# A two-layer convolution and attention block on one core: a new table of steps, rounded scores, a select on GpSimd and an FFN begun by halves

## The reference

```python
x = x + conv_attention(group_norm(x, 32 groups))   # rms norm over channels, 4 heads of 32, softmax over all 256 tokens
t = to_tokens(x)                                   # [4, 256, 64]
t = t + attention(layer_norm(t))                   # 4 heads of 16, causal mask, biases
t = t + moe_ffn(layer_norm(t))                     # 8 experts, 64 -> 256 -> 64, exact gelu, gate takes the top 2
x = from_tokens(t)
```

## Time and profile before

| | |
|---|---|
| median of 3 runs | 114.58 us |
| profiled execution, its own time | 114.85 us |
| its span (first to last instruction) | 112.8 us |
| PE busy | 101.8 us (90%) |
| DVE busy | 75.4 us (67%) |
| ACT busy | 65.1 us (58%) |
| GpSimd busy | 15.8 us (14%) |
| chain that ended last | PE 68%, DVE 16%, ACT 10%, issue 3% |
| granted clock of TensorE, mean | 0.998 |

### The profile page before, as it was taken

One profiled execution on the slowest core, in us unless ns is written; L12 is line 12 of the kernel. 1 busy time (PEld: TensorE's weight loads), 2 busy tenths in 40 slices (PEclk: granted clock), 3 DMA queues, 4 the chain that ended last, 5 costly groups with the idle time before them and its releaser, 6 DMA issues.

```text
span 112.8 us, 2251 instructions
## 1 busy us (share of the span) xinstructions
PE 101.8 (90%) x831; PEld 52.8 (47%) x831; DVE 75.4 (67%) x210; ACT 65.1 (58%) x121; POOL 15.8 (14%) x28
## 2 busy tenths in 40 slices
PE   5989978889899999997899998999999999999920
PEld 2346456655555455566666654675342323232300
DVE  6965899979505469999966688998638453155250
ACT  4039973433888756564329958894937644764400
POOL 7900200000000000000000000000003941343140
PEclk9999999999999999999999999999999999999999
DMA  2940000199700000000000000000000000000003
GB/s 74 246 84 7 2 0 9 31 237 189 118 0 0 0 9 0 0 0 0 6 0 6 0 0 0 0 0 3 0 6 0 0 0 0 0 0 0 0 0 93
DMA packets 6633, 3.16 MB, mean 28 GB/s; under 512 B 4432, under 2 KB 6496, under 8 KB 6624
## 3 DMA queue, kind: packets, MB, share of 16 engines
q1 hardware_dynamic: 5936, 2.38, 11.5%
q10 hardware_dynamic: 688, 0.66, 2.3%
HBM read 2.77 MB, written 0.26 MB: 27 GB/s over the span
## 4 chain that ended last, share of the span: by engine, by line
PE 68%; DVE 16%; ACT 10%; issue 3%; DVEq 0%; ACTq 0%
PE bank L933 13%; PE bank L944 13%; PE bank L874 6%; PE bank L807 6%; PE bank L839 5%; PE bank L888 4%; PE bank L858 4%; PE bank L749 3%; PE bank L758 3%; PE bank L721 2%; DVE mx L590 2%; DVE mx L586 2%; ACT sq L399 2%; PE bank L845 1%; ACT sq L405 1%
## 5 line engine op out<-in xcount | busy, mean ns | idle before, releaser
L481 ACT ACTIVATE hid<-bank,b1c 128x1024 f32<-128x1024 f32 x16 | 16.9, 1112 | 11.8 <-PE bank L933 11.8
L437 ACT ACTIVATE pr<-bank 128x1024 f32<-128x1024 f32 (+1 forms) x16 | 14.0, 914 | 8.5 <-PE bank L845 5.1
L933 PE MATMUL bank<-xn,w_sb 64*128 64x512 f32 x64 | 15.6, 612 | 0.0
L944 PE MATMUL bank<-hid,w_sb 128*64 128x512 f32 x64 | 15.3, 603 | 0.0
L705 DVE SCALAR_TENSOR_TENSOR yw<-bank,b2c,wc 128x512 f32<-128x512 f32 x8 | 6.0, 748 | 12.6 <-PE bank L944 12.6
L721 PE MATMUL bank<-still 128*128 128x512 bf16 (+1 forms) x41 | 11.8, 437 | 1.2 <-DVE still L495 1.2
L359 POOL TENSOR_TENSOR acc<-yw,x 64x512 f32<-64x512 f32 x1 | 1.3, 1269 | 72.1 <-DVE yw L705 72.1
L586 DVE TENSOR_REDUCE mx<-bank 128x4 f32<-128x1024 f32 x8 | 9.3, 1218 | 0.9 <-PE bank L807 0.8
L807 PE MATMUL bank<-k,q 32*128 32x256 f32 (+1 forms) x128 | 8.3, 373 | 1.6 <-ACT q L425 0.6
L933 PEld LDWEIGHTS bank<-xn,w_sb 64*128 64x128 f32 x64 | 5.6, 186 | 8.5 <-ACT hid L481 4.4
L364 POOL TENSOR_TENSOR acc<-acc,yw 128x512 f32<-128x512 f32 x6 | 7.6, 1274 | 11.8 <-DVE yw L705 11.6
(11 more groups left out here) (148 smaller groups left out, 176.4 us busy)
## 6 DMA issues: line engine op xcount, KB each, us to landing
w_sb<-in_L_ffn_W_dram SPq DMA_DIRECT2D x3, 512.0 KB, 7.2
x<-in_x_dram ACTq DMA_DIRECT2D x2, 256.0 KB, 4.8
xg<-in_x_dram SPq DMA_DIRECT2D x1, 256.0 KB, 3.2
wg<-in_L_conv_w_qkv_dram SPq DMA_DIRECT2D x2, 96.0 KB, 4.8
bqkv<-in_L_attn_b_qkv_dram SPq DMA_DIRECT2D x12, 0.1 KB, 1.6
wo1t<-in_L_attn_W_out_dram SPq DMA_DIRECT2D x8, 4.0 KB, 1.8
out_dram<-acc SPq DMA_DIRECT2D x1, 128.0 KB, 2.5
out_dram<-acc ACTq DMA_DIRECT2D x1, 128.0 KB, 2.8
```

The costliest lines, as they stand in the source:

```text
L437: nc.scalar.activation(pr[:, b, 2 * p:2 * p + 2, 0:n], two(key, 0, n), ACT.Exp, scale=SCALE[l]).then_inc(free(key), 1)
L481: nc.scalar.activation(hid[:, k % 4, :, :], two(("h", 0, k)), ACT.Gelu, bias=b1c[:, k:k + 1]).then_inc(free(("h", 0, k)), 1)
L933: i = mm(ps(key, i=s), w1_sb[r, e, P * j:P * j + P], XN[r, 2 * s:2 * s + 2, :].rearrange("p b t -> p (b t)"), start=True, stop=True)
L944: i = mm(ps(key, p0=C * s, p1=C * s + C), w2_sb[:, k, :], hid[:, k % 4, s, :], start=(j == 0), stop=(j == FT - 1))
```

## The change

The table of steps is new in every place and bank, and has a further column with the number of zero matmuls ahead of a step. Beside that:

- Queries and keys are copied a second time, to a rounded 32-bit format (fp32r), by GpSimd (steps `qr`, `kr`, tiles Qr and Kr). `scores` uses these; `again` goes on with the float32 ones. So `scores` waits for `qr` and `kr`.
- `turn` becomes a matmul in fp32r with a rounded identity (a further cast on DVE in the set-up) in place of a float32 transpose.
- In layer 1 the mask matmuls of `again` (L845) are gone. After each exp, GpSimd sets the masked weights to zero by a select (steps `causal0`, `causal1`, 512 elements in each partition), and `num` waits for both. One of the two mask tables in the set-up is gone.
- In layer 0 the sums of rows have a bank of their own (`pd`), with a semaphore of its own, so `inv` can begin before `num` is done.
- The FFN works on the batches as 0, 2 (upper half) and 1, 3 (lower half). The first three `up` are cut into two halves of 256 columns. The first halves (`uphalf`) need batches 0 and 1 only and stand in the table, at 253, 260 and 263, ahead of the last gate at 264; the second halves follow after it.
- Zero matmuls: 13 at the start as before, then 26 in place of 28. 2 are ahead of the first `var`, 1 and 1 ahead of the first two `project`, 9 more in layer 0 (3 `scores`, 3 `turn`, 2 `again`, 1 `den`), 12 in layer 1 (7 `scores`, 1 `turn`, 4 `out`), and 1 ahead of a gate.
- `prep_rest` (PE) and the two ACT set-up copies are steps of the table now.

The diff, cut to its core:

```diff
 PLAN = (
...
-    ("xr", 0, (9, 14, 23, 31), ()),
-    ("xn", 0, (12, 18, 27, 39), ()),
-    ("project", 0, (16, 29, 35, 46), ((3, 4), (4, 3), (2, 0), (6, 7))),
-    ("q", 0, (21, 33, 37, 48), ()),
-    ("k", 0, (22, 36, 42, 49), ()),
-    ("scores", 0, (25, 40, 50, 53), ((0, 6), (6, 2), (4, 2), (6, 0))),
-    ("max0", 0, (32, 44, 52, 57), ()),
-    ("max1", 0, (34, 45, 54, 61), ()),
-    ("turn", 0, (38, 56, 60, 66), ((4,), (5,), (5,), (0,))),
+    ("xr", 0, (7, 21, 40, 44), (), ()),
+    ("xn", 0, (10, 24, 45, 46), (), ()),
+    ("project", 0, (12, 29, 47, 49), ((0, 4), (6, 7), (6, 7), (2, 3)), (1, 1, 0, 0)),
+    ("q", 0, (17, 32, 51, 58), (), ()),
+    ("k", 0, (16, 37, 50, 55), (), ()),
+    ("qr", 0, (19, 34, 53, 61), (), ()),
+    ("kr", 0, (22, 41, 56, 59), (), ()),
+    ("scores", 0, (25, 54, 67, 77), ((4, 0), (0, 6), (6, 4), (4, 0)), (3, 0, 0, 0)),
+    ("max0", 0, (28, 57, 69, 79), (), ()),
+    ("max1", 0, (33, 62, 71, 83), (), ()),
+    ("turn", 0, (38, 65, 75, 88), ((6,), (0,), (7,), (3,)), (2, 0, 1, 0)),
...
-    ("xn", 2, (212, 217, 226, 232), ()),
-    ("gate", 2, (218, 222, 230, 234), ((7,), (2,), (7,), (2,))),
-    ("logits", 2, (221, 231, 233, 235), ()),
+    ("xn", 2, (235, 246, 254, 259), (), ()),
+    ("gate", 2, (240, 251, 258, 264), ((0,), (0,), (5,), (5,)), (0, 0, 1, 0)),
+    ("logits", 2, (244, 261, 262, 265), (), ()),
+    ("uphalf", 2, (253, 260, 263), ((6,), (2,), (0,)), (0, 0, 0)),
 )
...
+            def causal(l, b, p):
+                emptied(pool, ("t", l, b, p))
+                diag = pr[:, b, 2 * p:2 * p + 2, :].rearrange("p h (n c) -> p h n c", c=P)[:, :, 0:3:2, :]
+                nc.gpsimd.affine_select(out=diag, in_=diag, compare_op=ALU.is_ge, fill=0.0, base=0,
+                                        pattern=[[0, 2], [0, 2], [1, P]], channel_multiplier=-1).then_inc(S["causal", p], 1)
+            def qr(l, b):
+                emptied(pool, ("yq", l, b))
+                nc.gpsimd.tensor_copy(Qr[:, b, :], Q[:, b, 0:T]).then_inc(S["qr", l], 1)
+            def kr(l, b):
+                emptied(pool, ("yk", l, b))
+                nc.gpsimd.tensor_copy(Kr[:, b, :], K[:, b, 0:T]).then_inc(S["kr", l], 1)
...
+            nc.vector.tensor_copy(identr[:, :], ident[:, :]).then_inc(cst, 1)
...
             def scores(l, b):
...
-                emptied(pe, ("yq", l, b))
-                emptied(pe, ("yk", l, b))
+                idle(("s", l, b, 0), ZEROS["scores", l][b])
+                pe.wait_ge(S["qr", l], b + 1)
+                pe.wait_ge(S["kr", l], b + 1)
...
-                        i = mm(bank_of("s", l, b, h)(c, c + n), Q[rows(h), b, P * q:P * q + P], K[rows(h), b, 0:n],
+                        i = mm(bank_of("s", l, b, h)(c, c + n), Qr[rows(h), b, P * q:P * q + P], Kr[rows(h), b, 0:n],
...
             def turn(l, b):
-                    i = nc.tensor.transpose(ps(key, P * q, P * q + P), mx[l][:, b, q, :, :].rearrange("p h c -> p (h c)"), ident[:, :])
+                    i = mm(ps(key, P * q, P * q + P), mx[l][:, b, q, :, :].rearrange("p h c -> p (h c)"), identr[:, :],
+                           start=True, stop=True)
...
             def again(l, b):
...
-                if l:
-                    for h in range(H):
-                        i = mm(blocks(bank_of("t", l, b, h)(0, L1)), identb[:, :], twice(cmask[:, 1, :]), start=False, stop=True,
-                               skip_group_check=True)
...
+            def up_part(k, n):
+                key = ("h", 0, k)
+                if n == 0:
+                    claim(pe, key)
+                    idle(key, ZEROS["uphalf", 2][k])
+                pe.wait_ge(ld["w1"], 32)
+                pe.wait_ge(S["xn", 2], 2 * n + 2)
+                e, j = divmod(k, FT)
+                for s in range(2):
+                    r = slice(C * s, C * s + C)
+                    i = mm(ps(key, T * n, T * n + T, i=s), w1_sb[r, e, P * j:P * j + P], XN[r, 2 * n + s, :],
+                           start=(n == 0), stop=True, skip_group_check=True)
+                if n:
+                    i.then_inc(full(key), 1)
...
-            up(0)
-            up(1)
+            for k in range(3):
+                up_part(k, 1)
             pe.wait_ge(ld["w2"], 16)
             for e in range(E):
-                if e + 1 < E:
+                if e == 0:
+                    up(3)
+                elif e + 1 < E:
```

More of the change, by code:

```diff
@@ L42 @@
[L42 to L52, removed]
@@ L63 @@
[L63 to L72, removed]
@@ new lines @@
+    ("inv", 0, (64, 85, 106, 122), (), ()),
+    ("weigh", 0, (66, 87, 110, 126), (), ()),
+    ("out", 0, (72, 90, 116, 129), ((6,), (2,), (0,), (7,)), (0, 0, 0, 0)),
+    ("resid", 0, (74, 92, 124, 132), (), ()),
+    ("center", 1, (78, 94, 127, 135), ((6,), (7,), (0,), (1,)), (0, 0, 0, 0)),
+    ("square", 1, (82, 97, 130, 141), (), ()),
+    ("var", 1, (91, 99, 131, 144), (), ()),
+    ("ln", 1, (98, 111, 133, 148), (), ()),
+    ("r", 1, (100, 113, 136, 150), (), ()),
+    ("r2", 1, (104, 115, 138, 155), (), ()),
@@ new lines @@
+    ("den", 1, (188, 199, 210, 223), (), ()),
+    ("inv", 1, (191, 203, 214, 227), (), ()),
+    ("weigh", 1, (193, 206, 219, 232), (), ()),
+    ("out", 1, (198, 211, 224, 236), ((4,), (5,), (6,), (6,)), (2, 0, 0, 2)),
+    ("resid", 1, (202, 216, 229, 239), (), ()),
+    ("center", 2, (207, 221, 230, 243), ((4,), (5,), (1,), (4,)), (0, 0, 0, 0)),
+    ("square", 2, (212, 225, 237, 245), (), ()),
+    ("var", 2, (215, 228, 238, 248), (), ()),
+    ("ln", 2, (218, 231, 241, 252), (), ()),
+    ("r", 2, (220, 233, 247, 255), (), ()),
@@ L102, in hybrid_block @@
     ORDER = [(step, l, b, banks[b] if banks else ()) for _, step, l, b, banks in
-             sorted((place[b], step, l, b, banks) for step, l, place, banks in PLAN for b in range(B))]
+             sorted((at, step, l, b, banks) for step, l, place, banks, _ in PLAN for b, at in enumerate(place))]
+    ZEROS = {(step, l): zeros for step, l, _, _, zeros in PLAN}
     seat, nth, follows = {}, {}, {}
@@ L124, in hybrid_block @@
             take(("norm", l, b), banks[0])
+        elif step == "prept":
+            take(("prep_t", 0), banks[0])
         elif step == "project":
@@ L133, in hybrid_block @@
         elif step in ("den", "num") and banks:
-            take(("pv", l, b), banks[0])
+            take(("pd" if step == "den" else "pv", l, b), banks[0])
         elif step == "out":
@@ L138, in hybrid_block @@
             take(("logits", l, b), banks[0])
-    for k in range(NK):
-        take(("h", 0, k), 2 * (k % 3), 2)
-    take(("gate_t", 0), 7)
+        elif step == "uphalf":
+            take(("h", 0, b), banks[0], 2)
+    for k in range(3, NK):
+        take(("h", 0, k), seat["h", 0, k % 3], 2)
+    last_pair = 12 - sum(seat["h", 0, k] for k in range(3))
+    take(("gate_t", 0), last_pair + 1)
     for e in range(E):
-        take(("y", 0, e), 6 + e % 2)
+        take(("y", 0, e), last_pair + e % 2)
     with ExitStack() as ctx:
@@ L635, in logits @@
                 emptied(dve, key)
-                for t in range(KT * b, KT * b + KT):
+                for t in range(first, first + KT):
                     i = nc.vector.max(m8[:, t, :], lg[:, t, :])
@@ L830, in again @@
                     claim(pe, ("t", l, b, p))
+                idle(("t", l, b, 0), ZEROS["again", l][b])
                 emptied(pe, ("turn", l, b))
+                emptied(pe, ("yq", l, b))
+                emptied(pe, ("yk", l, b))
                 if l == 0:
@@ L880, in out_ @@
                 claim(pe, key)
+                idle(key, ZEROS["out", l][b])
                 w = wo0t[:, :] if l == 0 else wo1t[:, :, :].rearrange("p r c -> p (r c)")
@@ L892, in gate @@
                 claim(pe, key)
-                idle(key, (2, 2, 4, 4)[b])
+                idle(key, ZEROS["gate", l][b])
                 pe.wait_ge(S["xn", l], b + 1)
```

180 lines of the change are left out of this document (104 added, 76 removed).

## The result

The changed kernel takes 115.38 us (median of 5, 115.26 to 115.60) against 114.65 for the kernel before: the ratio is 1.0058, 95% interval 1.004 to 1.0076. It is slower, by 0.7 us or 0.6%, small but clear of the interval, where I forecast 4.0 us faster. (Ratios here leave out executions that were more than 1.5% above the fastest of their kernel; where that hides something, single times are given.)

What follows compares the result with a forecast made beforehand. PE was taken to bound the kernel, with DVE level in two stretches. Terms -4.3 + 1.3 + 0.6 + 0.5 - 0.9 - 1.2 = -4.0 took 114.85 to 110.85, less 0.27: 110.6 us; range 106.8 to 114.2.

Steps and rivals of the forecast that it cites:

- What of this lands: PE's work to the end of layer 1: 6.2 us leave PE, of which 4.3 were counted as gained.
- its hops: GpSimd's new copies and selects between steps, and what GpSimd holds up on DVE: 0.6 us cost, bounds 0 and 4.
- the masks' 2.2 us: Mask of `again` in layer 1: 0.54 us four times off PE, three of four where PE sets the pace.
- Scores: fp32r scores steps: 0.55 us in layer 0, 0.45 in layer 1; 2.4 and 1.6 us saved on PE.
- Turn: Transposes as fp32r matmuls, eight steps: no change taken, bounds -2.1 to +3.0 us.
- Prologue: Start of batch 0: scores at 15.2 us in place of 14.36, first maxima about 0.2 later; +0.5 in the sum.
- Zero matmuls: 22 come in from the second `project` to the end of layer 1: 1.3 us cost, from 0 to 4.8.
- Rival D: Clock falls in the prologue, PE at half speed from 12 to 20 us: 115.6 us, chance 0.07.
- Halves: Three halves of `up` moved ahead of the last gate, free in place of zero matmuls: 1.2 us gained.
- the rest of the last stretch: From `out` of batch 3 to the first `up`, 6.97 us: 0.9 us gained, bounds 0 and 1.2.
- Rival C: GpSimd's copies and selects hold up two-input DVE instructions; at 10 us of delay 116.6 us, chance 0.07.

Runs made afterwards that it cites:

- z_all: Kernel before, old order, with all edits but the own bank for the sums, and 14 zero matmuls more: 114.58 us, ratio 0.9984.
- b_select: Kernel before with one edit: GpSimd's select in place of the mask matmuls of the second scores; 114.55 us, ratio 0.9985.
- n_f32: Changed kernel with its first scores back in float32, without the 16 GpSimd copies: 118.64 us, ratio 1.0366 to the kernel before.
- n_mask: Changed kernel with the second mask on PE again and no select: 116.53 us, ratio 1.0182 to the kernel before.
- n_zerohalves: Changed kernel with two zero matmuls in place of each first half, first three up matmuls whole behind the last gate: 115.73 us.
- n_kr: Changed kernel with kr of batch 0 ahead of the copy of w_qk in GpSimd's queue, nothing else: 114.41 us.
- n_nozero: Changed kernel without its 26 zero matmuls past the opening 13: 117.76 us median, single times 116.04 to 119.25.
- b_scores: Kernel before with one edit: GpSimd copies queries and keys to fp32r for the first scores, old order and zeros; 115.65 us median.

## Why the prediction was wrong, point by point

- **The step that failed: "What of this lands", 4.3 of 6.2 us, with the new order itself priced only by its zeros, its hops and its prologue.** I argued from the old trace where PE's work was worth its time, and let the new table inherit that. In the old order with the clock held, all the edits together, halves included, give 0.2 us (z_all, with 14 zero matmuls more), and the masks' 2.2 us give 0.2 (b_select): the stretches at 98% PE give no time back, since the chain through exp, shuffle and `inv` ends just as late. The new order then costs 0.8 us more at nearly the same edits (115.38 against 114.58), a term that my sum did not have. Those two make up the 0.7 us, within the 0.2 us that such differences are good to. Inside the new table the same edits are worth 4.8 us (n_f32, n_mask, n_zerohalves), near my 4.3, but measured from a start that I never priced: the new table with the old work, some 120 us by that estimate.
- **Sizes of the edits: good.** Scores 0.44 us in place of my 0.55 and 0.45. Turn 0.37 to 0.41, I took no change. Copies 0.43 and 0.44 (0.42), selects 0.68 (0.85).
- **Prologue: start right, price wrong.** `kr` ended at 15.03 and the scores started at 15.17; I had 15.2. The first maxima came 0.1 late. But removing that wait gives 0.97 us at the end, since later work follows it one for one. I had compared it with the old start and not with what the faster prologue could have had (first maxima at 14.65, n_kr).
- **Zero matmuls: wrong in sign.** 1.3 us of cost in the sum; without them the kernel is 2.4 us slower by the medians. Rival D had the mechanism (less load on PE, 1.2 GHz, matmuls of nearly twice the length) and the place, 12 to 20 us: in n_nozero PE ran slow from 11.5 to about 25 us, in b_scores, which keeps the old zeros of the prologue, from 16.9 to 23.4. It did not befall the changed kernel, whose table has zeros ahead of the waits. I counted 12 of 16 zeros as gone by 14 us; three new ones run at 13.27, so it is 10. And the rows that I set against D begin at 14.4: asked from 1.19 to 6.84 us, the clock column reads 1.00 too, while the matmuls there took 0.435 us each. So at the start the column does not show the slow clock; in b_scores and n_nozero it does.
- **Halves: 1.2 predicted, 0.35 measured (n_zerohalves), -0.5 in the old order.** I left out that the fourth `up` waits for the first gelu to free its bank. They were not free either: one stands on the path ahead of the last gate, 0.70 us (77.78). And of the 0.9 for the rest of the last stretch next to nothing came: from the last `out` to the end of the last gate pass 6.92 us (72.11 to 79.03), were 6.97. In the last stretch as a whole, 0.6 us came where 2.1 were predicted.
- **Rival C, GpSimd holding up DVE: real and small.** `xn` stayed at 425 ns. `att` (L662, two SBUF inputs) went from 426 to 470 ns on average, by one of eight, which ran beside a select that began 0.13 us earlier (63.01):

```profile
63.14 0.78 DVE L662 SCALAR_TENSOR_TENSOR att<-dr,att 128x256 f32<-128x256 f32 x1
```

b_select has the same once: 0.78 us at 64.83, a select from 64.70. The Trainium skill (SBUF — State Buffer, "Who interferes with whom") states that a DVE instruction with two SBUF inputs contends with a GpSimd instruction that reads SBUF. These two cases agree, with a price near 0.4 us each; rival C had 10 us in all.
- **My range and chances.** 106.8 to 114.2 had no room for a table that is worse by itself; none of the rivals had that either.

Still open: that the new order loses 2.9 us at layer 0's second maxima and gains them back by 46 us was read from the traces but not tested; 0.3 to 0.4 of the 0.8 us between the two orders have no cause shown; the early `kr` was not run in the old order with the halves; and the own bank for the sums was never run by itself.

## What to carry to other kernels

Price a new order of steps apart from the edits that come with it: run the edits in the old order and the old work in the new one, since an edit's worth depends on the order (here 0.2 us in one, some 4.8 in the other). Before counting filler matmuls as waste, take them out and look at the granted clock of single executions; an edit that lightens PE can cost more in clock than it saves. And look at what the first operands of the prologue are queued behind on a side engine: here two set-up instructions, 0.90 us together (13.53 to 14.43), moved the whole kernel by 0.97.

## What the runs showed of the hardware

- One fp32r step of 8 matmuls of 256 columns on four row groups took 0.44 us where float32 took 1.08 to 1.21; an fp32r matmul against the identity took as long as a float32 transpose (0.37 to 0.41 for two).
- The granted clock fell in only some executions of one and the same kernel: b_scores took 113.83 to 118.56 us at means of 0.995 to 0.935. A single profile would have shown one of these. The kernel before fell too, but rarely: 3 of its 107 executions beside the experiments, at 0.981 and 116.2 to 116.5 us.
- The clock fell after waits of PE of no more than 1.22 and 0.50 us (b_scores, profiled execution), while in the kernel before, with waits of 0.41 and 0.57 us at the same places and scores of 1.15 us between in place of 0.51, it stayed at 1.00. The changed kernel waited 1.08 and 0.25 us there, after three zero matmuls, and stayed at 1.00 as well.
